# Self attention of a fused block: the head mask moves from the queries to the keys, and one score product of 400 columns replaces four of 100

## The reference, cut to what matters

```python
q = (src @ Wq).reshape(Bb, Tt, H, DH).transpose(0, 2, 1, 3)          # 16 heads of 16
k = (src @ Wk_c @ Wk).reshape(Bb, Tt, H, DH).transpose(0, 2, 1, 3)
v = (src @ Wv_c @ Wv).reshape(Bb, Tt, H, DH).transpose(0, 2, 1, 3)
q = _apply_rope(q, sin, cos)
k = _apply_rope(k, sin, cos)
attn = jnp.einsum('bhqd,bhkd->bhqk', q, k) / np.sqrt(DH).astype(np.float32)
attn = jax.nn.softmax(attn, axis=-1)
sa = jnp.einsum('bhqk,bhkd->bhqd', attn, v)
```

## Time and profile before

| what | value |
| --- | --- |
| median of 3 runs | 539.65 us |
| span of the profiled execution, first to last instruction | 534.7 us |
| PE busy | 500.6 us (94%), 3452 matmul records |
| DVE busy | 276.7 us (52%) |
| ACT busy | 187.7 us (35%) |
| POOL busy | 161.2 us (30%) |
| chain that ended last: PE, DVE | 78%, 11% |
| granted TensorE clock, mean | 0.987 |

### The profile page before, as it was taken

The page is one execution under the profiler, slowest core; times in us unless marked ns, Lnnn a source line. Parts: engine busy times, 40 slices in busy tenths (PEclk is TensorE's granted clock), DMA queues, the critical chain, the costliest instruction groups (busy, mean ns, idle before and its releaser), DMA issues.

```text
span 534.7 us, 9480 instructions
## 1 busy us (share of the span) xinstructions
PE 500.6 (94%) x3452; PEld 335.8 (63%) x3452; DVE 276.7 (52%) x664; ACT 187.7 (35%) x444; POOL 161.2 (30%) x180
## 2 busy tenths in 40 slices
PE   9989898999998969999999988899999899999991
PEld 8556654454566657788877767787866575444441
DVE  3466651221227475656676877988654226223352
ACT  2343231211114345555555564556662104200000
POOL 3130123011126044332231562543201467100242
PEclk9999999999999998999999999999999999999997
DMA  5999994499877697885664209400000153111100
GB/s 138 265 277 313 385 348 127 158 361 392 310 244 219 147 252 170 209 234 139 173 163 97 54 1 331 143 2 3 1 1 1 42 150 113 41 37 54 27 12 24
DMA packets 52588, 82.33 MB, mean 154 GB/s; under 512 B 10910, under 2 KB 41126, under 8 KB 52541
## 3 DMA queue, kind: packets, MB, share of 16 engines
q1 hardware_dynamic: 45788, 69.05, 43.5%
q0 software_dynamic: 5776, 12.13, 7.2%
q10 hardware_dynamic: 976, 0.53, 0.4%
HBM read 66.87 MB, written 15.15 MB: 153 GB/s over the span
## 4 chain that ended last, share of the span: by engine, by line
PE 78%; DVE 11%; issue 4%; DMA 2%; POOL 2%; ACT 2%; POOLq 0%; SPq 0%; DVEq 0%; ACTq 0%
PE pb L1551 72%; DVE hN L1111 1%; DVE nmx L1412 1%; POOL xs_dram L656 1%; DVE prob L1415 1%; PE pb L1990 1%; DMA hN<-yt_dram 1%; PE pb L1849 1%; PE pb L1759 1%; DVE ctxbuf L1342 1%; DVE nmx L1320 1%; PE pb L1561 1%; DVE x L1263 1%; PE pb L1723 1%; DMA xs_dram<-arena,slot 1%
## 5 line engine op out<-in xcount | busy, mean ns | idle before, releaser
L1551 PE MATMUL pb<-split 128*100 128x362 f32 (+2 forms) x320 | 77.3, 325 | 6.4 <-DVE nmx L1320 2.7
L1551 PE MATMUL pb<-ring,big 128*116 (+1 forms) x232 | 76.8, 578 | 0.0
L1320 DVE TENSOR_REDUCE nmx<-pb 100x1 f32<-100x361 f32 x128 | 62.7, 527 | 24.2 <-PE pb L1551 23.8
L1551 PEld LDWEIGHTS pb<-split 128*100 128x100 f32 (+2 forms) x320 | 54.7, 179 | 16.4 <-issue 5.7
L1551 PEld LDWEIGHTS pb<-ring,big 128*116 128x116 f32 (+1 forms) x232 | 31.2, 162 | 42.0 <-issue 40.9
L987 ACT ACTIVATE big<-pb 121x400 f32<-121x400 f32 (+1 forms) x96 | 48.1, 504 | 22.5 <-PE pb L1551 19.9
L721 POOL TENSOR_TENSOR shift<-consts,nmx 100x400 fp32r<-100x400 f32 x32 | 28.2, 882 | 77.6 <-DVE nmx L1320 77.5
L1551 PE MATMUL pb<-big,arena 121*32 121x100 f32 (+3 forms) x1072 | 47.9, 264 | 1.7 <-ACT arena L835 1.2
L1551 PEld LDWEIGHTS pb<-big,arena 121*32 121x32 f32 (+3 forms) x1072 | 29.1, 113 | 18.4 <-issue 6.9
L1551 PE MATMUL pb<-shift 100*121 100x400 f32 (+1 forms) x96 | 34.6, 361 | 0.0
L1551 PE MATMUL pb<-hT,wgu 128*128 128x400 f32 (+1 forms) x100 | 33.0, 469 | 1.3 <-DVE big L1205 1.0
(11 more groups left out here) (277 smaller groups left out, 839.7 us busy)
## 6 DMA issues: line engine op xcount, KB each, us to landing
ring<-in_L_ffn_gate_up_proj SPq DMA_DIRECT2D x12, 1024.0 KB, 9.5
split<-kx_dram SPq DMA_DIRECT2D x64, 181.0 KB, 4.1
ring<-in_L_ffn_down_proj SPq DMA_DIRECT2D x12, 512.0 KB, 7.6
kx_dram<-split POOLq DMA_DIRECT2D x16, 362.0 KB, 5.1
ctxbuf<-in_L_ffn_gate_up_proj SPq DMA_DIRECT2D x4, 1024.0 KB, 8.9
ring<-in_L_ffn_W_experts SPq DMA_DIRECT2D x4, 1024.0 KB, 12.7
ctxbuf<-in_ctxT SPq DMA_DIRECT2D x10, 361.0 KB
split<-qx_dram SPq DMA_DIRECT2D x64, 50.0 KB, 2.1
```

What stands on the lines that cost most here:

```text
L1320: nc.vector.tensor_reduce(nmx[:, t % 4, q:q + 1], PB[SB[n % 3]][0:T, 0:CTX], AX.X, ALU.max, negate=True) \
L1551: return nc.tensor.matmul(o, l, r, start=start, stop=stop)
```

## The change

The keys are spread by head (`kbd`, in the buffers that held `qbd`) and the queries stay as they are. Then the spread operand of four heads, 400 adjacent columns, can be the moving one, and the batch's queries of a half (100 columns) the stationary one for all four: one product in place of four, with the same values in the same places of the same bank. Since the first spread now needs keys, the first unit's pieces are made in the order C, K, K, Q, Q (before Q, Q, C, K, K) in the same steps, the first two rotations are those of keys, and the first three rotations stand one step later in DVE's list. The first spread stands one step later in POOL's. From the fifth on, the rotations keep their order and steps; the fourth keeps its step and is of queries instead of keys. The spreads of batches 4 and 5 now wait for rotation 5 (added at n = 11) instead of 4 (n = 7), those of batches 6 and 7 for rotation 7 (n = 21) instead of 6 (n = 17).

```diff
-EARLY_SELF = {(21, "middle"): ("g", 0, 0), (22, "middle"): ("g", 1, 0), (23, "middle"): ("Q", 0, 0), (24, "middle"): ("Q", 0, 1),
-              (24, "end"): ("C", 0, 0), (25, "middle"): ("K", 0, 0), (26, "middle"): ("K", 0, 1), (27, "middle"): ("V", 0, 0),
+EARLY_SELF = {(21, "middle"): ("g", 0, 0), (22, "middle"): ("g", 1, 0), (23, "middle"): ("C", 0, 0), (24, "middle"): ("K", 0, 0),
+              (24, "end"): ("K", 0, 1), (25, "middle"): ("Q", 0, 0), (26, "middle"): ("Q", 0, 1), (27, "middle"): ("V", 0, 0),
...
-ROTATE = [("q", 0), ("q", 1), ("k", 0), ("k", 1), ("q", 2), ("k", 2), ("q", 3), ("k", 3)]
-ROTATE_SWAP = [24, 25, 26, 30, NQUAD + 5, NQUAD + 8, NQUAD + 14, NQUAD + 18]
-ROTATE_SINE = [24, 26, 27, 30, NQUAD + 6, NQUAD + 9, NQUAD + 15, NQUAD + 19]
-ROTATE_ADD = [26, 28, 29, NQUAD + 1, NQUAD + 7, NQUAD + 11, NQUAD + 17, NQUAD + 21]
+ROTATE = [("k", 0), ("k", 1), ("q", 0), ("q", 1), ("q", 2), ("k", 2), ("q", 3), ("k", 3)]
+ROTATE_SWAP = [25, 26, 27, 30, NQUAD + 5, NQUAD + 8, NQUAD + 14, NQUAD + 18]
+ROTATE_SINE = [25, 27, 28, 30, NQUAD + 6, NQUAD + 9, NQUAD + 15, NQUAD + 19]
+ROTATE_ADD = [27, 29, 30, NQUAD + 1, NQUAD + 7, NQUAD + 11, NQUAD + 17, NQUAD + 21]
...
-            def spread_queries(b):
-                pool.wait_ge(s("d_rot"), ROTATE.index(("q", b // 2)) + 1)
+            def spread_keys(b):
+                pool.wait_ge(s("d_rot"), ROTATE.index(("k", b // 2)) + 1)
                 if b >= 2:
                     pool.wait_ge(s("d_s"), 4 * (b - 1))
-                q = qT[:, :, T * b:T * b + T].unsqueeze(2).to_broadcast([128, KT, 8, T])
+                keys = krT[:, :, T * b:T * b + T].unsqueeze(2).to_broadcast([128, KT, 8, T])
...
-                if t == 29:
-                    spread_queries(0)
+                if t == 30:
+                    spread_keys(0)
...
-                        pe.wait_ge(s("d_qbd"), b + 1)
-                        pe.wait_ge(s("d_rot"), ROTATE.index(("k", b // 2)) + 1)
+                        pe.wait_ge(s("d_kbd"), b + 1)
+                        pe.wait_ge(s("d_rot"), ROTATE.index(("q", b // 2)) + 1)
                     if n >= 3:
                         pe.wait_ge(s("d_max"), n - 2)
-                    for q in range(4):
-                        h = 4 * g + q
-                        last = mm(PB[SB[n % 3]][0:T, T * q:T * q + T], qbd[:, b % 2, h // 8, T * (h % 8):T * (h % 8) + T],
-                                  krT[:, h // 8, T * b:T * b + T], True, True)
-                    last.then_inc(s("d_s"), 1)
+                    mm(PB[SB[n % 3]][0:T, 0:4 * T], qT[:, g // 2, T * b:T * b + T],
+                       kbd[:, b % 2, g // 2, 4 * T * (g % 2):4 * T * (g % 2 + 1)], True, True).then_inc(s("d_s"), 1)
```

More of the change, by code:

```diff
@@ L284, in build @@
         vpad = carve(0, VBUF, NJ, NH * 32)
-        qbd = ctxbuf[:, 0:QBD].rearrange("p (u k n) -> p u k n", u=2, k=KT)
+        kbd = ctxbuf[:, 0:QBD].rearrange("p (u k n) -> p u k n", u=2, k=KT)
         att_n = big[0:T, 0:2 * D].rearrange("p (u d) -> p u d", u=2)
@@ L398, in build @@
                   "c_diag", "c_st", "c_p", "c_av", "c_avsb", "c_turn", "c_att", "c_attT", "c_y", "c_res"]
-        names += ["d_kvc", "d_kvcsb", "d_k", "d_ksb", "d_swap", "d_cos", "d_rot", "d_qbd", "d_v", "d_vsb", "d_s", "d_max", "d_p",
+        names += ["d_kvc", "d_kvcsb", "d_k", "d_ksb", "d_swap", "d_cos", "d_rot", "d_kbd", "d_v", "d_vsb", "d_s", "d_max", "d_p",
                   "d_pt", "d_ptsb", "d_av", "d_att", "d_y", "d_x2", "d_sq",
@@ L682, in _ @@
             value_pads(range(2, VBUF))
-            def spread_queries(b):
-                pool.wait_ge(s("d_rot"), ROTATE.index(("q", b // 2)) + 1)
+            def spread_keys(b):
+                pool.wait_ge(s("d_rot"), ROTATE.index(("k", b // 2)) + 1)
                 if b >= 2:
                     pool.wait_ge(s("d_s"), 4 * (b - 1))
-                q = qT[:, :, T * b:T * b + T].unsqueeze(2).to_broadcast([128, KT, 8, T])
+                keys = krT[:, :, T * b:T * b + T].unsqueeze(2).to_broadcast([128, KT, 8, T])
                 m = consts[:, cs["headmask"]].unsqueeze(1).unsqueeze(3).to_broadcast([128, KT, 8, T])
-                nc.gpsimd.tensor_tensor(qbd[:, b % 2].rearrange("p k (h t) -> p k h t", h=8), q, m, ALU.mult) \
-                    .then_inc(s("d_qbd"), 1)
+                nc.gpsimd.tensor_tensor(kbd[:, b % 2].rearrange("p k (h t) -> p k h t", h=8), keys, m, ALU.mult) \
+                    .then_inc(s("d_kbd"), 1)
             def times_cos(r):
@@ L742, in _ @@
                         times_cos(r)
-                if t == 29:
-                    spread_queries(0)
+                if t == 30:
+                    spread_keys(0)
             times_cos(3)
-            spread_queries(1)
+            spread_keys(1)
             inverse_root("d", only=2)
-            spread_queries(2)
+            spread_keys(2)
             times_cos(4)
-            spread_queries(3)
+            spread_keys(3)
             times_cos(5)
-            spread_queries(4)
+            spread_keys(4)
             times_cos(6)
-            spread_queries(5)
+            spread_keys(5)
             times_cos(7)
-            spread_queries(6)
-            spread_queries(7)
+            spread_keys(6)
+            spread_keys(7)
             inverse_root("e")
```

## The result

The changed kernel takes 544.93 us (median of 12 runs, 542.08 to 546.93), beside 540.02 us for the kernel before in as many. The ratio is 1.0076, 95% interval 1.0053 to 1.0098: **slower by 4.1 us** by that ratio. The ratios here leave disturbed runs out, and the one profile of such a run (experiment 6) is read only in a stretch with the clock in full. In a second measurement it was 1.0082 (1.0051 to 1.0114). The forecast was +1.4 us, with 542.5 as the range's upper end.

What follows compares the result with a forecast made beforehand. Self attention was taken as bound by DVE and PE first, then by PE, with the end of cross attention mattering as much; -0.7 - 0.3 + 2.4 = +1.4 us gave 541.0 us, range 537.8 less 0.1 to 542.5.

Steps and rivals of the forecast that it cites:

- the likeliest case: Whole kernel: the forecast itself, +1.4 us to 541.0 us, given a chance of 0.55.
- term 3: End of cross attention: DVE held up by the moved instructions and spread, PE's last score product late, +2.4 us.
- (a): Add, sine and shuffle ahead of the maxima of t = 30: PE's product begins at 310.65, not 309.66.
- (d): Maxima of t = 31 begin at 316.2, not 313.84; PE's product goes from 314.41 to about 316.8, +2.4 us.
- (b): POOL's diagonal tile gets in between DVE's two normalised rows at about 312.0 and ends at about 312.95.
- (c): The spread follows the tile to 315.8; DVE's sine meets it at about 313.0 and ends at 316.2.
- Term 1: Self-attention scores: one wider product saves 0.03 us a step in 18 steps, plus 0.2 us at hand-overs, -0.7 us.
- Term 2: Self attention, spread of batch 4: it no longer stretches DVE's add from 0.57 to 2.30 us, -0.3 us.
- the sine or the row did not get ahead of the spread: Rival, end of cross attention: sine or second row runs before the spread, sum -1.3, 538.3 us; chance 0.27.
- the root did not get in between: Rival: inverse root gets between add and sine ahead of the maxima of t = 30, +2.0, 541.7 us; chance 0.10.
- nothing was bound by the number of products: Rival judged: self-attention score group bound by product count, sum -7.5, 532.2 us; chance 0.02.
- PE's wait did not fit into its old ones: Rival judged: no visible change, the new wait fits PE's old 0.46 and 1.43 us, 539.6 us; chance 0.06.

Runs made afterwards that it cites:

- experiment 6: Changed kernel with the first spread one POOL tile later, its 400-column score product again four of 100: ratio to before 0.9958, self attention 67.48 against 67.01 us.
- Run 2: Changed kernel plus 14 unread products on PE in the gap before its last cross-attention score product: ratio to before 1.0031, repeated 1.0060.
- run 5: Changed kernel with the sine ahead of the maxima of step 31 moved behind them: ratio to before 1.0109, PE's wait 2.43 us.
- run 7: Kernel before with the spread of batch 4 also waiting for rotation 5: self attention 67.50 us, ratio to before 1.0017.

## Why the prediction was wrong

The sign of the likeliest case was right; the size was not: +1.4 us forecast, +4.1 measured.

- **The step that failed** is the last one of term 3: "PE's product goes from 314.41 to about 316.8: +2.4 us". It prices a wait by its length alone and lets everything behind it run as before. I had read that the clock was granted in full there and took it for given, though by my own walk PE was about to stand still for about twice as long. The clock fell to 1.2 GHz in the wait and stayed there for 6.8 us, 5.5 of them behind the wait, and the stretch to self attention took 2.24 us more. Run 2 shows the cause: with the same lateness and PE at work, the second stretch is back at 10.15 and 10.16 us in both profiles. No rival held it either, so the range was too short above.
- **Steps (a) to (d)**: +2.52 us from t = 25 to t = 31, against 2.4. (a) was +1.0 and measured +0.93 (23.88 us from the maxima of t = 25 to those of t = 30, against 22.95). The root waited for the add and the sine, as I took it to. (b) came true: the tile got in between the two rows. (c) was wrong in who is stopped: I sent the second row through and let the sine meet the spread. It was the row, from 313.1 to just behind the spread's end (3.77 us), and the sine came after it in 0.56 us. The end of both is nearly the same, so the sum didn't suffer, but moving the sine, which my step would have had as the cure, cures 0.55 us (run 5).
- **Term 1**: -0.7 forecast, -0.47 by run 6. The pair saved 0.02 to 0.03 us a step, as read; the 0.2 us for the hand-overs were not seen apart. The number of products doesn't bound that group: four times as many cost 0.47 us in 32 steps. The Trainium skill's gap per matmul (TensorE: Matmul & The Clock Gate, "Back-to-back issue gap"), by which the term would have been some -8 us by an estimate, doesn't hold for these: one product in place of four brought the transposes 0.02 us closer (0.68 against 0.70 us).
- **Term 2**: -0.3 forecast, -0.40 by run 7.
- Terms 1 and 2 together were -1.0, and self attention took 0.91 less. What I costed at nothing cost nothing: the spread of batch 6 was in time.
- **The rivals**: the sine or the row did not get ahead of the spread; the root did not get in between; nothing was bound by the number of products; PE's wait did not fit into its old ones.
- **Two readings of the profile before were off**, without moving the sum. The 4.95 us between its span and the median don't lie around the span: in all executions with both numbers 1.9 to 2.0 us do (543.23 us for a span of 541.3), so the execution that I read was some 3 us faster than the median one. And the clock wasn't granted in full from 186.9 us on: it was at half for 3.4 us from 200.2, and again close to the end. From 283 to 394 us it was in full, as the argument needs.
- Left open: the rest between 3.85 us of the stretches and the 4.1 of the ratio, which is within its interval, and how often the other pieces at half clock come. That they come more often after the change wasn't shown.

## What to carry to other kernels

A wait of PE in work that PE bounds costs its length and then, perhaps, the clock behind it: for any change that makes one PE wait some microseconds longer, look at what follows at half clock before settling the sum. A long instruction on POOL that stops DVE belongs where nobody waits for DVE; one tile further down the list the same 2.9 us cost nothing. And when whole times scatter by 1%, stretches between fixed instructions at a known clock repeat within 0.1 us.

## What the runs showed of the hardware

- The granted clock fell in all four profiles in which PE stood still for 2.4 to 3.1 us ahead of its last score product (3.04 us and 6.8 us at half clock in the changed kernel, 6.8 again in its repetition, 2.92 and 3.4, 2.43 and 3.4), and in none of the ten in which it waited there for at most 1.44 us at a time or was given work. It fell between 1.7 us into the wait and 1.3 us behind its end. The price was 1.2 to 2.7 us. What makes the piece 6.8 us long in one kernel and 3.4 in another isn't shown.
- A POOL instruction that is queued behind another can keep DVE out for both. The second row began at 313.1, in the tile's time, and had to wait for the spread as well, which began only at 313.81. In the three profiles shown with this row (changed, before with the late spread, sine behind the maxima) the spread began right at the tile's end, ahead of the waiting row. It isn't a rule: in the kernel before, where the tile is queued behind the spread (309.56 to 312.42, then the tile to 313.28), the first row ended 0.15 us after the spread, well ahead of the tile's end:

```profile
310.84 1.73 DVE L1111 TENSOR_SCALAR hN<-x,mv,rstd 100x256 f32<-100x256 f32 x1
```

What decides it isn't shown.
